# Paged attention in four stages on one core: six of eight heads with scores from halves, transposes three heads behind, and ScalarE copying three of eight transposed weights

## What is computed

```python
kc = k_cache[block_table].reshape(bsz, L, HK, D)          # 64 batches, L = 512 cached keys, 8 key heads, D = 128
k_all = jnp.concatenate([kc, k], axis=1)                  # and 32 new keys: 544
...
rep = HQ // HK                                            # 32 query heads, 4 to a key head
scores = jnp.einsum('bqhd,bkhd->bhqk', q, k_all) * SCALE
scores = jnp.where(valid[:, None, None, :], scores, -1e+30)
probs = jax.nn.softmax(scores, axis=-1)
o = jnp.einsum('bhqk,bkhd->bqhd', probs, v_all)
```

## Time and profile before

| | |
|---|---|
| median of 3 runs | 2338.12 us (2337.94 to 2339.78) |
| the profiled execution, its own time | 2333.55 us |
| its span | 2331.7 us |
| mean granted clock of TensorE | 0.985 |
| busy: TensorE | 2248.5 us (96%) |
| VectorE | 1760.6 us (76%) |
| ScalarE | 1331.9 us (57%) |
| GpSimd | 1161.4 us (50%) |
| data moved | 501.72 MB, 215 GB/s over the span |

### The profile page before, as it was taken

One profiled execution on the slowest core, in us unless ns is written; L12 is line 12 of the kernel. 1 busy time (PEld: TensorE's weight loads), 2 busy tenths in 40 slices (PEclk: granted clock), 3 DMA queues, 4 the chain that ended last, 5 costly groups with the idle time before them and its releaser, 6 DMA issues. The chain is left out here.

```text
span 2331.7 us, 52504 instructions
## 1 busy us (share of the span) xinstructions
PE 2248.5 (96%) x16512; PEld 1950.0 (84%) x16512; DVE 1760.6 (76%) x3503; ACT 1331.9 (57%) x2643; POOL 1161.4 (50%) x1218
## 2 busy tenths in 40 slices
PE   7998999999994999999999999999999997999999
PEld 6877777777773999999999999999999996888887
DVE  8851788888884999999999999999999996422222
ACT  6833888888873666666665666666666654311111
POOL 4200444544543777777777777777777773000000
PEclk9999999999996999999999999999999998999999
DMA  7633343443436888888888888888888885643442
GB/s 264 211 109 104 91 129 112 132 129 124 126 113 214 284 293 295 291 294 293 288 286 285 289 288 294 291 294 292 294 295 289 288 294 172 206 133 95 137 129 63
DMA packets 451815, 501.72 MB, mean 215 GB/s; under 512 B 95861, under 2 KB 390773, under 8 KB 443414
## 3 DMA queue, kind: packets, MB, share of 16 engines
q1 hardware_dynamic: 414870, 366.44, 49.7%
q0 software_dynamic: 36864, 134.23, 16.3%
HBM read 408.21 MB, written 92.34 MB: 215 GB/s over the span
## 5 line engine op out<-in xcount | busy, mean ns | idle before, releaser
L1120 POOL TENSOR_TENSOR att_probs<-att_probs,att_inverse 128x512 f32<-128x512 f32 x512 | 535.1, 1045 | 268.6 <-DVE att_inverse L1316 263.9
L1224 ACT ACTIVATE att_probs<-att_probs,att_low 128x544 f32<-128x544 f32 x512 | 383.8, 750 | 474.2 <-DVE att_low L1303 401.0
L1181 PE MATMUL att_o<-att_probs_t,att_values 128*128 128x128 f32 x4096 | 547.3, 277 | 0.0
L1181 PEld LDWEIGHTS att_o<-att_probs_t,att_values 128*128 128x128 f32 x4096 | 497.4, 192 | 8.6 <-issue 0.2
L1303 DVE CUSTOM_DVE_ANT_0 att_probs<-att_score,att_mask,att_batch_cols 128x544 f32<-128x544 f32 x512 | 398.5, 778 | 74.7 <-PE att_score L1151 55.9
L1312 DVE COPY att_probs_t<-att_turn 128x512 f32<-128x512 f32 x512 | 350.6, 685 | 1.2 <-PE att_turn L1161 1.2
L1106 POOL DMA_INDIRECT att_values<-L_cond_v_cache,att_v_rows_of x256 | 298.3, 1165 | 82.5 <-POOL att_v_rows_of L1102 50.1
L1279 DVE TENSOR_TENSOR att_keys_lo<-att_keys_raw,att_keys_hi 128x480 fp32r<-128x480 f32 (+1 forms) x320 | 321.5, 1006 | 17.4 <-ACT att_keys_hi L1217 17.4
L1161 PE MATMUL att_turn<-ident,att_probs 128*128 128x128 f32 x2048 | 311.2, 274 | 1.2 <-POOL att_probs L1120 0.8
L958 POOL TENSOR_TENSOR proj_q_out<-proj_by_cos,proj_by_sin 128x512 f32<-128x512 f32 x128 | 188.1, 1470 | 216.5 <-DVE proj_by_sin L886 216.5
L1161 PEld LDWEIGHTS att_turn<-ident,att_probs 128*128 128x128 f32 x2048 | 241.7, 141 | 27.7 <-POOL att_probs L1120 1.4
(11 more groups left out here) (129 smaller groups left out, 3920.9 us busy)
## 6 DMA issues: line engine op xcount, KB each, us to landing
att_keys_raw<-L_cond_k_cache SPq DMA_DIRECT2D x1024, 128.0 KB
q_t<-proj_q_out SPq DMA_DIRECT2D x32, 1024.0 KB, 5.3
att_queries_raw<-q_t SPq DMA_DIRECT2D x64, 512.0 KB
o_t<-att_heads_out SPq DMA_DIRECT2D x64, 512.0 KB, 7.8
out_o_raw<-o_t SPq DMA_DIRECT2D x32, 1024.0 KB, 5.8
maps_even<-L_cond_weight SPq DMA_DIRECT2D x8, 1024.0 KB, 12.6
maps_odd<-L_cond_weight SPq DMA_DIRECT2D x8, 1024.0 KB, 16.9
w_nat<-L_cond_Wq SPq DMA_DIRECT2D x8, 1024.0 KB, 6.4
```

Source lines behind the costliest of these rows:

```text
L1120: nc.gpsimd.tensor_tensor(probs[:, k, 0:L], probs[:, k, 0:L], inverse[:, k:k + 1].to_broadcast([P, L]), ALU.mult).then_inc(probs_ready, 1)
L1181: last = nc.tensor.matmul(o, values[j][:, t, h * D:(h + 1) * D], probs_t[m % 2][:, t * P:(t + 1) * P], start=(t == 0), stop=False, skip_gr ...
L1224: nc.scalar.activation(probs[:, k, :], probs[:, k, :], ACT.Exp, bias=low[k][:, 0:1], scale=-1.0, accum_out=total[k][:, 0:1]).then_inc(exp_ ...
```

## The change

- `NATIVE` goes from 3 to 2: six of eight heads are split, so a part of three pages has 576 columns; the keys are cut into six parts (five of three pages, the last of two with 384 columns), and the query part has 768 columns.
- The parts begin earlier: ScalarE in the step of head 1 (was 3), VectorE in that of head 2 (was 4). The keys' buffer is loaded again one head earlier, since the first split head is number 2.
- `LAG`: transposes are of head n - 3 (was n - 2), weighing of head n - 4 (was n - 3). The new keys' transposes move from the steps of heads 1 and 5 to those of 2 and 6, the new values' multiplications from 2 and 6 to 3 and 7.
- ScalarE copies the transposed weights of heads 1, 4 and 7 (`KEPT_BY_ACT`), ahead of the softmax of the step; VectorE keeps the other five.
- ScalarE's `new_part` and `keep_o` move one step later, GpSimd's gathers from the steps of heads 3 to 6 to those of 4 to 7.

```diff
--- before.py
+++ after.py
@@ -971,10 +971,13 @@
     GH = 4
     RING = 8
     PAIRS = B // 2
-    NATIVE = 3
-    ACT_FROM, DVE_FROM = 3, 4
+    NATIVE = 2
+    ACT_FROM, DVE_FROM = 1, 2
+
+    LAG = 3
+    KEPT_BY_ACT = (1, 4, 7)
     SPLIT = HK - NATIVE
-    PARTS = [slice(0, 3), slice(3, 6), slice(6, 9), slice(9, 13), slice(13, NPP + 1)]
+    PARTS = [slice(0, 3), slice(3, 6), slice(6, 9), slice(9, 12), slice(12, 15), slice(15, NPP + 1)]
     NP = len(PARTS)
     FIRST = NPP // 2 + 1
     LEFT = 512 - FIRST * PSIZE
@@ -1110,11 +1113,11 @@
             def pair(i, first, last_pair):
                 for n in range(N):
                     j, h = divmod(n, HK)
-                    if 3 <= h < 3 + PPT and not (last_pair and j == 1):
-                        if h == 3 and (j or not first):
+                    if 4 <= h < 4 + PPT and not (last_pair and j == 1):
+                        if h == 4 and (j or not first):
 
                             pool.wait_ge(o_done, i * N + j * HK)
-                        load((j + 1) % 2, i * 2 + (j + 1), h - 3)
+                        load((j + 1) % 2, i * 2 + (j + 1), h - 4)
                     pool.wait_ge(inverse_ready, i * N + n + 1)
                     k = n % RING
                     nc.gpsimd.tensor_tensor(probs[:, k, 0:L], probs[:, k, 0:L], inverse[:, k:k + 1].to_broadcast([P, L]),
@@ -1193,18 +1196,17 @@
             def pair(i, first):
                 for n in range(N):
                     scores(i, n)
-                    if n >= 2 or not first:
-                        turn(i, n - 2)
-                    if n >= 3 or not first:
-                        weigh(i, n - 3)
+                    if n >= LAG or not first:
+                        turn(i, n - LAG)
+                    if n > LAG or not first:
+                        weigh(i, n - LAG - 1)
 
             pair(0, True)
             with pe.Fori(1, PAIRS) as i:
                 pair(i, False)
-            turn(PAIRS, -2)
-            weigh(PAIRS, -3)
-            turn(PAIRS, -1)
-            weigh(PAIRS, -2)
+            for n in range(-LAG, 0):
+                turn(PAIRS, n)
+                weigh(PAIRS, n - 1)
             weigh(PAIRS, -1)
 
         @block.scalar
@@ -1223,6 +1225,13 @@
                 k = n % RING
                 nc.scalar.activation(probs[:, k, :], probs[:, k, :], ACT.Exp, bias=low[k][:, 0:1], scale=-1.0,
                                      accum_out=total[k][:, 0:1]).then_inc(exp_done, 1)
+
+            def main_part(i, n):
+                m = n % N
+                back = i if n >= 0 else i - 1
+                act.wait_ge(turned, i * N + (n + 1))
+                act.wait_ge(weighed[m % 2], back * (N // 2) + m // 2)
+                nc.scalar.activation(probs_t[m % 2][:], turn_ps[:], ACT.Copy).then_inc(kept, 1)
 
             def new_part(i, n, first=False):
 
@@ -1249,6 +1258,8 @@
             def pair(i, first, last_pair):
                 for n in range(N):
                     j, h = divmod(n, HK)
+                    if (n - LAG) % HK in KEPT_BY_ACT and (n >= LAG or not first):
+                        main_part(i, n - LAG)
                     softmax(i, n)
                     if HK - ACT_FROM + h <= NP:
                         split(i * 2 + j, i, HK - ACT_FROM + h, j)
@@ -1257,10 +1268,10 @@
 
                             act.wait_ge(scores_done, i * N + j * HK)
                         split(i * 2 + (j + 1), i + j, h - ACT_FROM, (j + 1) % 2)
-                    if n % GH == 1 and (n >= GH or not first):
-                        new_part(i, n - 2, first)
                     if n % GH == 2 and (n >= GH or not first):
-                        keep_o(i, n - 3)
+                        new_part(i, n - LAG, first)
+                    if n % GH == 3 and (n >= GH or not first):
+                        keep_o(i, n - LAG - 1)
 
             for c in range(HK - ACT_FROM):
                 split(0, 0, c, 0)
@@ -1268,6 +1279,9 @@
             with act.Fori(1, PAIRS - 1) as i:
                 pair(i, False, False)
             pair(PAIRS - 1, False, True)
+            for n in range(-LAG, 0):
+                if n % HK in KEPT_BY_ACT:
+                    main_part(PAIRS, n)
             new_part(PAIRS, -1)
             keep_o(PAIRS, -1)
 
@@ -1319,8 +1333,8 @@
                 for n in range(N):
                     j, h = divmod(n, HK)
                     mask_scores(i, n, first)
-                    if n >= 2 or not first:
-                        main_part(i, n - 2)
+                    if (n >= LAG or not first) and (n - LAG) % HK not in KEPT_BY_ACT:
+                        main_part(i, n - LAG)
                     if HK - DVE_FROM + h <= NP:
                         split(i * 2 + j, HK - DVE_FROM + h, j)
                     if not (last_pair and j == 1):
@@ -1345,8 +1359,9 @@
             with dve.Fori(1, PAIRS - 1) as i:
                 pair(i, False, False)
             pair(PAIRS - 1, False, True)
-            main_part(PAIRS, -2)
-            main_part(PAIRS, -1)
+            for n in range(-LAG, 0):
+                if n % HK not in KEPT_BY_ACT:
+                    main_part(PAIRS, n)
 
 
 def stage_output(nc, wo, ident, ot_dram, x3_dram, out):
```

## The result

The changed kernel takes 2392.24 us (median, 2389.59 to 2393.82) where the kernel before takes 2338.03: a ratio of 1.0233, 95% interval 1.0215 to 1.0250. It is slower by 54 us; the forecast was slower by 17 us, with 2368 as the upper end. So the sign was right and the size was three times too small.

A forecast was written before the change was run, and what follows sets the result against it. TensorE was taken to bound the kernel, VectorE close behind. A floor of 18.49 us plus pauses of 0.18, 0.48 and 0.04 gave 19.19 us per batch; with +1 us at start and end, 2355 us, range 2316 to 2368.

The forecast's parts named there:

- The bound and the floor: TensorE sets the pace; without new pauses a batch falls from 18.94 to 18.49 us.
- One native head less, transposes later: TensorE saves 0.16 us per batch; head 6's 0.12 us pause for GpSimd's multiplication goes.
- The long head moves, and heads 6 and 0 pay: New-value matmuls move to heads 7 and 3, so head 6 no longer absorbs VectorE's delay; pauses of 0.18 and 0.48 us.
- the pause in head 6: TensorE waits 0.18 us before head 7's scores because VectorE's mask of head 6 is late.
- So mult(4) stands where it stood against T5: GpSimd's multiplication of head 4, 0.58 us later, keeps its place against T5 (head 5's scores start), with T3 to T5 0.60 longer.
- the collision in step 5: VectorE's subtraction during head 5 stands still beside GpSimd's multiplication of head 4, taking 1.2 us.
- The pause in head 0: TensorE waits 0.48 us in head 0: late mask of head 7, so ScalarE frees the output banks late.
- The sum: Batch period 18.49 + 0.18 + 0.48 + 0.04 = 19.19 us, 0.25 more than before; +16.8 us in all.
- The exclusive lock: VectorE's subtraction stands still beside a GpSimd multiplication, save a 0.11 us start, ending 0.53 us after it (480 columns).
- the strict rule: VectorE's whole subtraction would follow GpSimd's multiplication, 0.12 us later than in the trace; 2362 us.
- Rival A (not blocked): VectorE's subtractions at the tight heads escape GpSimd's multiplications; period 18.55 us, 2315 us; chance 0.22.
- Rival B (keys late): ScalarE's key split waits for late key loads, 1 us per batch; 2418 us; chance 0.05.

The follow-up runs named there:

- experiment 9: Changed kernel with index copy moved to head 2's step, gathers in steps of heads 4, 6, 7 and 0, output banks copied before the query half: 2319.63 us.
- experiment 4: Changed kernel in which GpSimd multiplies only 16 of a head's 512 weights by the reciprocal: 2343.79 us.
- experiment 6: Changed kernel with three native heads and the old parts and first steps; longer lag, ScalarE's three copies and later gathers stay: 2382.07 us.
- experiment 3: Changed kernel in which ScalarE copies the transposed weights of heads 2, 3 and 7 instead of 1, 4 and 7: 2365.9 us.
- experiment 1: Changed kernel with GpSimd's index copy moved from just before the first gather to the step of head 2: 2338.51 us.
- experiment 5: Changed kernel with the index copy in head 2's step and gathers issued in the steps of heads 4, 6, 7 and 0: 2325.83 us.
- experiment 7: Changed kernel with a lag of 2 again, new-key copies, bank copies and gathers in their old steps, wider halves kept: 2367.71 us.

## Why the prediction was right or wrong

- *The bound and the floor.* Right. The floor was put at 18.49 us; experiment 9, where no mask is late, has 18.59. Head 4 is 0.07 us longer than a plain split head (0.04 was predicted, as a pause), and in head 0 the scores after the new values take 0.1 us more (1317.22 to the transposes at 1318.24 in the changed kernel, against 0.92 us in head 1).
- *One native head less, transposes later.* Right in size, 0.16 us. Without the transposes of the new keys (0.11) and the new values (0.61), head 1 went from 2.25 us to 2.17, since a split head now follows it, and head 2 from 2.17 to 2.09. No transposes wait for GpSimd any more.
- *The long head moves, and heads 6 and 0 pay.* Right in mechanism, and shown: experiment 4 shortened the multiplications, the pause in head 6 went and 0.10 us was left of that in head 0; experiment 6 went back to the narrow halves and kept the lag, ScalarE's copies and the later gathers, and both stayed.
- *"So mult(4) stands where it stood against T5".* This is the step that failed. It added 0.58 us for the copy and its gather, with the copy at its old 0.18 us. I left out what VectorE does beside the copy in its new place. VectorE's copy of head 1 has gone to ScalarE, so the subtraction of step 4 starts 1.88 us after T4 instead of 2.46, just ahead of the copy of the indices (T4 + 2.02). The copy took 0.71 us, as the median of all 64. Multiplication 3 to multiplication 4 was forecast at 3.39 us and measured 3.86. With that the collision in step 5 goes from partial to whole: the subtraction takes 1.61 us and not 1.2, and the pause in head 6 was 0.57 us instead of 0.18. Experiment 3 shows it: there the copy takes 0.18 us, multiplication 4 starts at T5 + 1.97 where the prediction had T5 + 1.96, and the pause in head 6 is 0.17 us. Its time, 2365.9 us, is inside the forecast's own range. Experiment 1 takes away the whole copy with the wait behind it, and so all of the 54 us.
- *The pause in head 0.* 0.56 us instead of 0.48. Its chain (late mask 7, softmax, query half, banks) came step by step as written; mask 7 was at T7 + 1.73 instead of 1.61. With mask 7 on time the prediction left a pause of 0.02 us there; experiment 5 has 0.10.
- *The sum.* Pauses of 0.70 us were forecast, 1.20 came; the period is 19.74 instead of 19.19. That is 0.55 x 63 = 35 of the 37 us that the forecast was short. Of the 2 us that remain, 1.5 lie at the start and the end of the attention, which were put at 1 us: from the first scores to those of head 1 it takes 5.35 us instead of 3.90, and from the last batch's head 1 to the end of the weighing 22.48 instead of 21.46, 2.5 us in all.
- *The range.* It let each pause be 0.1 us off. The same subtraction, that of step 5, took 0.75 us in experiment 1, 1.61 here and up to 1.90 in experiment 7, so the bound for a term of this kind was too narrow.
- *The exclusive lock.* The Trainium skill, page "SBUF — State Buffer", section "Who interferes with whom", says that the loser fully blocks. The trace agrees but for 0.12 us: a subtraction of 576 columns that meets a multiplication ends 0.61 to 0.63 us after it, whatever part of it lay ahead, where it takes 0.75 alone. So the prediction's 0.53 us for 480 columns held; the strict rule's 2362 us lies nearer to the measured time, but for a reason that the trace doesn't show. The section also says that issue order decides who blocks. The records here don't bear that out by their starts: experiment 3 has subtractions of 576 columns that start up to 0.20 us ahead of the multiplication and still stand still for all of it. Whether the multiplication had been issued earlier than its record starts, no run shows.
- *Rival A (not blocked).* The multiplications did fall elsewhere, but half a microsecond the wrong way. Where the masks are on time the time is 2326 us (experiment 5) and 2320 (experiment 9), not far above the rival's 2315.
- *Rival B (keys late).* Wrong for the changed kernel, whose ScalarE waits for no keys in the steady state. In experiment 4, 1 us per batch below it, they are late in half of the batches; in experiment 5, at the same pace, they are not.

## What to carry to other kernels

When one engine's step is moved by a head, ask for every short instruction of VectorE and GpSimd what it now lies beside on the other of the two, the index copies too: here a copy of 4 columns in the wrong place, with the wait of its gather, cost 54 us of 2338. Taking a copy off one engine can be what moves its next instruction into such a place. A long head (extra matrix work) is slack for whoever is late in it; moving it by one step moves the slack, so late work must move with it. And a wait that is last hides the next: taking one away is worth little until the one behind is known.
